# A transformer's last stage: which engine reads the query/key bank first, ScalarE's square or VectorE's rotary products

## The reference, cut to what matters

```python
def attn_layer(x, Wqkv, qs, ksc, Wo):
    q, k, v = jnp.split(x @ Wqkv, 3, -1)          # 16 heads of 64
    q = l2norm(q) * qs                            # needs the sum of squares of every head
    k = l2norm(k) * ksc
    q = q * cos * scale + rotate_half(q) * sin * scale
    k = k * cos * inv + rotate_half(k) * sin * inv
    out = local_attention(q, k, v)                # windows of 64, each sees itself and the one before
    return out @ Wo
def ffn_layer(x, g, bln, W1, b1, W2, b2):
    xn = layernorm(x) * g + bln
    a, gate = jnp.split(xn @ W1 + b1, 2, -1)
    return a * gelu(gate) @ W2 + b2
for i in range(6):
    x = attn_layer(shift_tokens(x), ...) + x
    x = ffn_layer(shift_tokens(x), ...) + x
```

## Time and profile before

| | |
|---|---|
| median of 3 runs | 4751.27 us (4749.82 to 4754.07) |
| the profiled execution, its own time | 4754.24 us |
| its span, first to last instruction | 4752.9 us |
| last_part, from its first to its last instruction | 2126 to 4753 us, 384 tiles |
| PE busy (matmuls) | 4566.6 us, 96% |
| DVE, ACT, POOL busy | 3600.3, 3168.7, 2602.8 us |
| granted clock of PE, mean | 0.989 |

### The profile page before, as it was taken

How to read it: one execution, slowest core, us unless ns; L and a number is a source line. 1 busy time by engine, 2 the same in 40 slices (tenths; PEclk the granted TensorE clock), 3 DMA queues, 4 the chain that set the end, 5 groups by cost and what they waited for, 6 DMA issues and landing times.

```text
span 4752.9 us, 94769 instructions
## 1 busy us (share of the span) xinstructions
PE 4566.6 (96%) x35816; PEld 3007.9 (63%) x35816; DVE 3600.3 (76%) x6388; ACT 3168.7 (67%) x7744; POOL 2602.8 (55%) x2346
## 2 busy tenths in 40 slices
PE   6999999999999999969999999999999999999998
PEld 2333333334444343328888888888888888888887
DVE  4767666666666758858888888888888888888885
ACT  3666566555555555647777777777777777777774
POOL 3322211112121222129988888888888888887883
PEclk8999999999999999989999999999999999999999
DMA  5323323322222323301111111111111111111111
GB/s 121 67 51 60 72 45 64 71 58 52 59 41 51 66 54 58 57 28 50 45 40 40 41 41 38 42 41 36 39 44 41 40 39 40 40 37 38 39 45 31
DMA packets 178934, 233.20 MB, mean 49 GB/s; under 512 B 29648, under 2 KB 121424, under 8 KB 178256
## 3 DMA queue, kind: packets, MB, share of 16 engines
q1 hardware_dynamic: 178480, 227.14, 21.2%
HBM read 150.09 MB, written 32.51 MB: 38 GB/s over the span
## 4 chain that ended last, share of the span: by engine, by line
PE 78%; DVE 11%; ACT 4%; issue 3%; POOL 3%; DMA 1%; SPq 0%; DVEq 0%; ACTq 0%; POOLq 0%
PE psum L1449 16%; PE psum L1493 15%; PE psum L541 5%; PE psum L527 5%; PE psum L506 5%; PE psum L1535 4%; PE psum L1501 4%; PE psum L1525 3%; PE psum L1516 3%; PE psum L488 2%; DVE maxes L731 2%; PE psum L530 2%; PE psum L1511 2%; PE psum L496 2%; DVE sums L764 1%
## 5 line engine op out<-in xcount | busy, mean ns | idle before, releaser
L941 ACT ACTIVATE probs<-psum 128x1024 f32<-128x1024 f32 x610 | 621.6, 1023 | 449.3 <-PE psum L527 259.8
L731 DVE TENSOR_REDUCE maxes<-psum 128x1 f32<-128x1024 f32 x512 | 618.1, 1216 | 278.0 <-PE psum L506 274.2
L1764 ACT ACTIVATE lprobs<-psum,small_stats,stats 128x128 f32<-128x128 f32 x1536 | 688.9, 477 | 21.9 <-DVE small_stats L1652 21.0
L1822 POOL TENSOR_TENSOR stats<-stats,minus_half 128x8 f32<-128x8 f32 x384 | 680.2, 1771 | 32.0
L1493 PE MATMUL psum<-wqkv_hi,xs_hi 128*128 128x512 f32 (+1 forms) x1536 | 540.7, 352 | 17.7 <-POOL xs_lo L1809 16.4
L1818 POOL TENSOR_TENSOR lwork<-lwork 128x512 f32<-128x512 f32 x384 | 512.0, 1333 | 80.9 <-DVE lwork L1636 79.4
L527 PE MATMUL psum<-stack 98*128 98x512 bf16 x1536 | 502.9, 384 | 22.9 <-DVE maxes L731 12.2
L1493 PE MATMUL psum<-wqkv_lo,xs_hi 128*128 128x512 f32 (+1 forms) x1536 | 518.0, 337 | 0.0
L1493 PE MATMUL psum<-wqkv_hi,xs_lo 128*128 128x512 f32 (+1 forms) x1536 | 518.0, 337 | 0.0
L506 PE MATMUL psum<-stack 96*128 96x512 bf16 x1536 | 473.3, 385 | 32.6 <-ACT probs L938 10.0
L728 DVE CUSTOM_DVE_ANT_0 psum<-psum,mask_by_query 128x1024 f32<-128x1024 f32 x256 | 314.8, 1231 | 217.8 <-PE psum L506 216.2
(11 more groups left out here) (244 smaller groups left out, 11841.3 us busy)
## 6 DMA issues: line engine op xcount, KB each, us to landing
mixed_vals<-vals SPq DMA_DIRECT2D x672, 64.0 KB, 2.0
stack<-k_parts SPq DMA_DIRECT2D x288, 128.0 KB
staged<-in_quads SPq DMA_DIRECT2D x144, 256.0 KB, 2.9
k_parts<-parts SPq DMA_DIRECT2D x48, 384.0 KB, 2.9
stack<-q_parts SPq DMA_DIRECT2D x288, 64.0 KB
staged<-in_w SPq DMA_DIRECT2D x54, 256.0 KB, 3.0
ctx<-in_ctxT SPq DMA_DIRECT2D x24, 512.0 KB, 5.2
q_parts<-parts SPq DMA_DIRECT2D x24, 384.0 KB, 3.2
```

The lines of the kernel that those rows point to most:

```text
L731: ins = vector.tensor_reduce(to, pair(("M", u)), AX.XY, ALU.max)
L941: scalar.activation(probs[:, i % 6, :, :], pair(("E", u)), ACT.Exp).then_inc(S_["E_act"], 1)
L1764: ins = scalar.activation(pr[:, h, :], scores(u)[:, h % 2, h // 2, :], ACT.Exp, bias=st[:, 4 + h:5 + h], scale=y[:, h:h + 1], accum_out=st ...
L1822: pool_step(gpsimd.tensor_tensor(st[:, 8:16], st[:, 0:8], minus_half[:, :], ALU.pow))
```

## The change

ACT now squares the query/key bank as soon as `qk_pe` comes, ahead of the copy of the values. DVE's products no longer wait for `qk_pe` but for `sq_act`, that is, for the square. The bank is left with the last product (`qkv_dve`) where it was left with the square. The order of the banks, the buffers and all other stages stay as they were, and no instruction is added or removed.

```diff
-        LEAVES = {"qkv": ("sq_act", "qkv_act"), "tr": ("tr_act",), "pt": ("pt_act",), "pv": ("pv_dve",),
+        LEAVES = {"qkv": ("qkv_dve", "qkv_act"), "tr": ("tr_act",), "pt": ("pt_act",), "pv": ("pv_dve",),
...
                     V.wait_ge(S_["rt_dve"], at_("rt", d))
-                    V.wait_ge(S_["qk_pe"], at_("qkv", u))
+                    V.wait_ge(S_["sq_act"], at_("qkv", u))
                     left(work_at, ("t1", u), V)
...
                     d, g, b, tt = u
+                    A.wait_ge(S_["qk_pe"], at_("qkv", u))
+                    left(work_at, ("sq", u), A)
+                    scalar.activation(buf("sq", u), bank(("qkv", u, 0)), ACT.Square).then_inc(S_["sq_act"], 1)
                     A.wait_ge(S_["qkv_pe"], at_("qkv", u))
                     left(val_at, ("v", u), A)
                     heads = lambda ap: ap.rearrange("p (h d) -> p h d", h=4)
                     scalar.activation(vals[:, val_at["v", u][0], :, 0:LHD], heads(bank(("qkv", u, 1))[:, 0:256]), ACT.Copy).then_inc(S_["qkv_act"], 1)
-                    A.wait_ge(S_["qkv_dve"], at_("qkv", u))
-                    left(work_at, ("sq", u), A)
-                    scalar.activation(buf("sq", u), bank(("qkv", u, 0)), ACT.Square).then_inc(S_["sq_act"], 1)
```

## The result

The changed kernel takes 4783.41 us (median of 4 runs, 4783.20 to 4783.71) against 4750.55 us for the kernel before, run beside it (4 runs, 4749.66 to 4754.07): a ratio of 1.0067, 95% interval 1.0052 to 1.0082, 32.9 us slower. Forecast were 4786 us and a layer of 437 to 438 us; a layer takes 437.4 us. The profiled execution has a span of 4782.2 us against 4752.9, 29.3 us more; its first part, which the change doesn't touch, happens to be 2.6 us shorter than that of the profile before, which makes 31.9. So the two agree.

What follows compares the result with a forecast made beforehand. The prediction took PE to bound the kernel, busy 429.9 of a layer's 432.0 us. Its terms, 20 + 8 + 3 + 7 - 2 = +36 us on 4751.3, gave 4787, stated as 4786 us, with a range of 4755 to 4818.

Steps and rivals of the forecast that it cites:

- place A: Turn behind a gate's second product: late square and products delay PE's output projection by 0.9 us, 22 times, 20 us.
- place B: A gate followed by the short turn without feed-forward: PE 0.7 us late, 11 times in the run, 8 us.
- gates without a rounding: Three gates per layer with 1.6 us of DVE idle time: 0.1 us each, some 3 us with the token roundings.
- place C: First layer before its feed-forward, 32 turns: a closed loop over ACT and DVE lengthens turns, taken as 7 us.
- waits for the square won: PE's waits for the square elsewhere go in part: 2 us won of at most 10.9.
- (b, c): Products wait for the square, delaying DVE's later work (b); the bank comes 1.38 us after a late ACT (c).
- Faster: Rival: ACT comes free earlier and DVE's waiting for the projection absorbs its delay; 4740 us, chance 0.10.
- no change: Rival: place A's first 0.5 us is met, its second turn and place B absorbed; 4748 to 4760 us, chance 0.14.
- third rival: One more rounding falls under a POOL instruction at every place A and place B: 28 us more, 4815 us, chance 0.16.

Runs made afterwards that it cites:

- e3: Changed kernel, but neither engine waits for the other: the square reads a constant instead of the bank, so the norms are wrong; 4736.37 us, ratio 0.9969.
- p4: Kernel before, with POOL's remainder of the hidden values (L1842) cut to four elements; 4741.21 us, ratio 0.9976.
- p5: Changed kernel, with POOL's remainder of the hidden values (L1842) cut to four elements; 4771.28 us, ratio 1.0038.
- e2: Changed kernel, with ACT's copy of the values ahead of the square again, products still waiting for the square; 4849.39 us, ratio 1.0209.
- k4: Kernel before, with POOL's scaling of the keys (L1825) cut to four elements; 4738.52 us, ratio 0.9971.
- k5: Changed kernel, with POOL's scaling of the keys (L1825) cut to four elements; 4761.58 us, ratio 1.0018.
- g1: Kernel before, with the square first only in the 72 tiles projected in a turn with a gate; 4762.33 us, ratio 1.0024.
- e5: Changed kernel, but in a gate's turn ACT squares between its two Gelus, not behind both; 4764.11 us, ratio 1.0024.
- h1: Kernel before, with the square first only in 16 of a layer's 64 tiles, where DVE comes late to the products anyway; 4743.18 us, ratio 0.9982.
- h2: Kernel before, with the square first in 17 chosen tiles of 64, turn 33 added to the 16 where DVE comes late; 4740.52 us, ratio 0.9975.

## Why the prediction was right, and where it was not

The terms of the sum, in us for the whole run (per layer times 5.5, as many layers as the 22 places A and 11 places B of the prediction make; the first layer's start by itself):

| term | expected | measured |
|---|---|---|
| place A | +20 | 3.4 x 5.5 = +19 |
| place B | +8 | -0.13 x 5.5 = -1 |
| gates without a rounding | +3, with the next | 1.29 x 5.5 = +7 |
| turns 23, 39, 55 | in the above | 0.75 x 5.5 = +4 |
| place C (the first 36 turns) | +7 | +4.6 |
| waits for the square won | -2 | inside place A (turn 34) |
| sum | +36 | +34; 33.4 by the ends of the projections |

**The square and the products in one chain (b, c).** Right, and it is the cause of the loss: e3 takes the chain away and the loss with it. That the bank is left 1.38 us after the later of the two engines is free is what place A shows after.

**Place A: +20 us expected, 3.6 per layer; 3.4 measured** (0.86 + 1.49 - 0.38 + 1.44). The first turn is the step as told: 0.42 to 0.48 against 0.53, four times per layer (0.49, 0.48, 0.89, 0.47). The second turn was told wrongly in three ways. The last link of the chain was not the one that counted: I had the exponentials, the copy L1770 and its bank hold the output projection, but PE had lost 0.67 at L1525 and 0.42 at the projection (L1493, for L1663) before it came there, and the output projection added nothing. I let DVE's work between keep its durations; at turns 17 and 49 the rounding L1618 grows from 0.51 to 1.17 us under POOL's L1830, and each of these places costs 1.4 to 1.5 instead of 0.9. And I counted four equal places: at turn 34 the kernel before had a long wait for the square, and the change wins 1.26 us there. Its row in the trace of before:

```profile
3597.96 0.63 PE L1525 MATMUL psum<-ident,lprobs 128*128 128x128 f32 x4 [1.07 <-ACT lwork L1745]
```

That is a gain of the kind that I had priced at 2 us for the whole run; here alone it is 1.26 per layer, 7 us in the run. The costs above and this gain cancel, so the agreement of 19 with 20 us is in part luck.

**Place B: +8 us expected, nothing measured.** The step that failed: "The exponentials of 3458.09 wait for DVE and move by 0.64". The linear half was 0.45 late, near enough; but the rounding behind it shrank by as much:

```profile
3469.44 1.40 DVE L1702 SCALAR_TENSOR_TENSOR lwork<-psum,vecs,lwork 128x512 f32<-128x512 f32 x2
...
3472.20 2.71 POOL L1842 TENSOR_TENSOR hid_lo<-lwork,hid_hi 128x512 fp32r<-128x512 f32 x2
3472.69 1.07 DVE L1618 CAST wqkv_hi<-staged 128x512 fp32r<-128x512 f32 x1
...
3474.60 0.46 ACT L1764 ACTIVATE lprobs<-psum,small_stats,stats 128x128 f32<-128x128 f32 x1 [1.01 <-DVE small_stats L1652]
```

In the earlier trace rows L1618 takes 1.48 us from 3455.77. With PE's delay of 16.57 us its end would be 3473.82; it is 3473.76, though it started 0.35 late. The exponentials start at 3474.60, where 3458.09 + 16.57 = 3474.66 was on time. p4 and p5 add that without L1842 the lateness would have been swallowed too, by ACT, which is free earlier. It is a matter of size: in e2, where the products are later still, these turns lose 1.02 us per layer.

**Gates without a rounding: 0.1 each expected, 0.43 measured**, 1.29 per layer, 7 us in the run. The step: "1.6 us idle", from which I concluded that DVE would be on time. It was. POOL wasn't, and it lay across DVE's next cast (k4 and k5). The wrong assumption was that a delay reaches PE only through the engine that is delayed. To it belong the turns 23, 39 and 55, where I had seen only two roundings of the tokens (L1735) at 0.2 each: 0.75 per layer, 4 us in the run. At turn 39 PE waits 0.70 us for the bank of the products (0.26 us of idle time there before); 23 and 55 I haven't followed.

**Place C: +7 us expected, 4.6 measured** by turn 36. The loop is there: after, the scores of the turn of the earlier trace rows stand 5.54 us apart instead of 4.60, and PE waits for the exponentials.

```profile
2269.12 0.30 PE L1511 MATMUL psum<-band_bias,ident_b 64*64 64x256 bf16 x4
2274.66 0.30 PE L1511 MATMUL psum<-band_bias,ident_b 64*64 64x256 bf16 x4 [1.06 <-ACT lprobs L1764]
```

Eight turns grow by 0.4 to 0.9 each, half of the 16 that I allowed, and others give some back (turn 21: -0.8). The 7 was a choice between the loop's 4 and the 8 to 18 without anything given back, and was 50% high; what sets how many turns grow I haven't followed.

**The rivals.** Faster and no change needed the delay to be absorbed; of the places that I named it is at place B only. The third rival's mechanism, a rounding under POOL's instruction, is real at turns 17 and 49 (+0.66 each) and as L1709 at turns 10, 26 and 58 (+0.41 each), but it also gives back at turns 13, 34 and 45, which I hadn't thought of: I had it as a cost only. The Trainium skill, in SBUF — State Buffer, section Who interferes with whom, describes the port pair of the two engines as an exclusive lock where the second to come blocks; the rows shown here agree: in each, the cast that starts inside a POOL instruction ends 0.2 to 0.3 us after that instruction does. Read so, the rule says where time comes back too. It doesn't hold for every POOL instruction: casts inside L1822 are not held (last section), and there the measurement decides.

**What would have shown me wrong** was named as: a layer of 432 us or less, or L1702 without idle time and the scores on time. The second happened at place B, and place B was the part that was wrong.

**Turn 32 and what stays open.** The first turn of turns 32 to 35 loses 0.89 us in the changed kernel and 0.87 in g1, but nothing in e5. Between k4 and k5 it loses 0.49, between p4 and p5 0.46, as the other three do, so the second half of it hangs on POOL. The trace after shows how: the rounding ahead of this gate starts inside POOL's L1818 and takes 0.79 us (0.45 in e5, 0.42 in k5), the exponentials wait 0.32 us for the biases behind it and start 0.45 late against PE, and ACT goes from them without a pause to the Gelus, which end 0.43 later. Of the 13.5 us by which k4 is faster than before, some 4 come before turn 36 and 1.8 per layer later; only a part of them has a place in my table. That the two engines could read one bank at once was not tried.

## What to carry to other kernels

Where two engines read one buffer in turn, let the one go first that is idle when the data comes, tile by tile: the fixed new order costs 33 us here, the chosen one wins 7.4 (h1), and 11.5 with the one product that is made late at turn 33 (h2). A wait that moves an engine by 0.6 us also moves whoever works from its output, so ask for each delayed instruction not only who waits for it but what its successor on GpSimd will lie across. And read a loss by the ends of the same instruction in both traces, turn by turn: a sum that is right by total may be right for the wrong places, and PE's idle time showed only half of a layer's loss.

## What the runs showed of the hardware

A cast or subtraction of DVE that works in SBUF has no fixed time: L1618 takes 0.41, 0.51, 0.69, 0.82, 0.89, 1.07, 1.17 or 1.48 us, the same 128x512 elements, by where it starts in POOL's instruction, and L1712 0.69 to 1.66 us. But it depends on which instruction that is. In the last part of the trace before, 129 roundings start inside one of POOL's; 93 are stretched (0.46 to 1.5 us), and each of these ends 0.28 to 0.29 us after it. The 30 that start inside L1822, the power on 128x8 elements (1.7 us and more), all take 0.41 to 0.43 us, as if POOL were idle; so do 6 others. The products, which read PSUM, take 0.69 and 0.41 us in all these rows, also in the middle of a POOL instruction. A later start can leave the end nearly where it was: against the end of the same turn's projection, the rounding of place B starts 0.8 us later in e2 than before and ends 0.2 later, since it takes 0.89 us instead of 1.48. And POOL's own instructions stretch too, though less (L1825 0.61 to 1.15 us in the trace before), so neither side's mean can be used for a single place.
